# Loading Wk and the first context in three pieces, running the first four K tiles a chunk at a time, and moving Wv ahead of x

## The reference

```
q = LN(x) @ Wq.T + bq;  k = ctx @ Wk.T + bk;  v = ctx @ Wv.T + bv      # 16 heads of 32
x = x + (softmax(q k^T / sqrt(32) + mask) v) @ Wo.T + bo
x = x + self_attention(LN(x))           # q and k RMS-normalised per head
x = x + experts(LN(x))                  # 9 paths, one chosen per token by argmax, then a layer norm
```

## Time and profile before

| | us |
|---|---|
| median of three runs | 752.56 |
| the profiled execution, device time | 751.71 |
| its span, first to last instruction | 749.9 |
| outside the span | 1.81 |
| TensorE busy in the span | 708.2 (94%) |
| VectorE, ScalarE, GpSimd busy | 375.8, 339.7, 197.7 |
| the first matmul starts at | 10.03 |

### The profile page before, as it was taken

How to read it: one execution, slowest core, us unless ns; L and a number is a source line. 1 busy time by engine, 2 the same in 40 slices (tenths; PEclk the granted TensorE clock), 3 DMA queues, 4 the chain that set the end, 5 groups by cost and what they waited for, 6 DMA issues and landing times. The chain is left out here.

```text
span 749.9 us, 20567 instructions
## 1 busy us (share of the span) xinstructions
PE 708.2 (94%) x8150; PEld 550.0 (73%) x8150; DVE 375.8 (50%) x993; ACT 339.7 (45%) x743; POOL 197.7 (26%) x281
## 2 busy tenths in 40 slices
PE   4999999999999999999999999998999989788994
PEld 3777787787788778778778778786787777564662
DVE  5455334424424424425334434576568777581675
ACT  3535534535435434444444443543354544541663
POOL 0001001001001001001000011048776775535755
PEclk9999999999999999999999999999999999989997
DMA  8211110110110110110110211251000005348930
GB/s 332 86 56 58 58 50 9 58 56 0 56 56 0 56 56 0 56 56 0 56 56 5 51 56 38 75 136 10 17 15 28 29 31 199 103 164 303 347 137 31
DMA packets 17557, 55.97 MB, mean 75 GB/s; under 512 B 6098, under 2 KB 6354, under 8 KB 14566
## 3 DMA queue, kind: packets, MB, share of 16 engines
q1 hardware_dynamic: 13926, 40.64, 15.9%
q0 software_dynamic: 3584, 14.69, 5.1%
HBM read 46.93 MB, written 10.49 MB: 77 GB/s over the span
## 5 line engine op out<-in xcount | busy, mean ns | idle before, releaser
L96 PE MATMUL pj<-W_both 128*128 128x512 f32 x544 | 222.1, 408 | 10.1 <-DVE W_both L595 10.0
L98 PE MATMUL pj<-W_both 128*128 128x512 f32 x544 | 213.8, 393 | 0.0
L97 PE MATMUL pj<-W_both 128*128 128x512 f32 x544 | 212.7, 391 | 0.0
L96 PEld LDWEIGHTS pj<-W_both 128*128 128x128 f32 x544 | 102.8, 189 | 43.2 <-issue 23.6
L98 PEld LDWEIGHTS pj<-W_both 128*128 128x128 f32 x544 | 102.6, 189 | 23.0
L236 POOL COPY q_b<-Q_T 128x128 f32 (+1 forms) x32 | 9.3, 290 | 416.3 <-PE tp L359 349.3
L97 PEld LDWEIGHTS pj<-W_both 128*128 128x128 f32 x544 | 103.0, 189 | 19.2
L493 ACT ACTIVATE K<-pj,bk 128x512 f32<-128x512 f32 x64 | 44.1, 689 | 136.4 <-PE pj L98 136.4
L654 DVE CUSTOM_DVE_ANT_0 m_flat<-sc,mask 128x257 f32<-128x257 f32 x64 | 24.7, 424 | 116.5 <-PE tp L359 95.2
L508 ACT ACTIVATE p_flat<-m_flat,nmax 128x257 f32<-128x257 f32 x128 | 63.8, 501 | 25.5 <-DVE nmax L654 25.4
L500 ACT ACTIVATE V<-pj 128x512 f32<-128x512 f32 x64 | 38.2, 596 | 73.3 <-PE pj L98 71.8
(11 more groups left out here) (365 smaller groups left out, 1149.7 us busy)
## 6 DMA issues: line engine op xcount, KB each, us to landing
raw<-ctx_dram SPq DMA_DIRECT2D x15, 1024.0 KB, 4.8
experts<-w_dram SPq DMA_DIRECT2D x6, 768.0 KB, 5.8
raw<-w_dram SPq DMA_DIRECT2D x4, 1024.0 KB, 4.9
x_nat<-x_dram SPq DMA_DIRECT2D x2, 1024.0 KB, 12.1
rows<-z3s SPq DMA_DIRECT2D x8, 256.0 KB, 2.0
rows<-x_nat SPq DMA_DIRECT2D x8, 256.0 KB, 3.1
rows<-xm SPq DMA_DIRECT2D x8, 256.0 KB, 2.2
raw<-wk_dram SPq DMA_DIRECT2D x2, 512.0 KB, 5.7
```

Of the source, the lines that this page charges most:

```text
L96: eng.matmul(out, a_hi, b_hi, start=first, stop=False)
L97: eng.matmul(out, a_lo, b_hi, start=False, stop=False)
L98: return eng.matmul(out, a_hi, b_lo, start=False, stop=last)
```

## The change

The first loads come as a quarter (chunk 0), a quarter (chunk 1) and a half (chunks 2 and 3), each of `Wk` and of context 0 in turn; both splitting engines take the same three pieces. TensorE runs chunk 0 of all four K tiles, then chunk 1 of all four, and then tile by tile chunks 2 and 3. For that the four K tiles have a bank each: `pj[0]`, `pj[1]`, `sc[0]` and `sc[1]`. `Wv` is loaded right after, ahead of `bq`, `bk` and `x`; ScalarE splits it before it empties the first K tile, and VectorE before the layer norm statistics. V tile 0 waits for `Wv` chunk by chunk; V tiles 0 and 1 wait for K tiles 0 and 1 to be emptied, and `tails`, which uses `sc[0]` and `sc[1]` next, for K tiles 2 and 3. Two semaphores get a second use, with their later counts raised to match.

```diff
+        first_k_bank = (pj[0], pj[1], sc[0], sc[1])
-        in_halves = (slice(0, CT // 2), slice(CT // 2, CT))
+        in_parts = (slice(0, 1), slice(1, 2), slice(2, CT))
@@ SyncE
-            for i, half in enumerate((slice(0, CT * D // 2), slice(CT * D // 2, CT * D))):
-                eng.dma_start(raw[:, 1, half], io["wk"][:, half]).then_inc(wk_in[i], 16)
-                eng.dma_start(p_flat[:, half], io["ctx"][0][:, half]).then_inc(ctx_in[0] if i else ctx0_in, 16)
-            eng.dma_start(x_nat[:, 0:4, :], io["x"][:, 0:4, :]).then_inc(x_in[0], 16)
+            for i, cs in enumerate(in_parts):
+                part = slice(cs.start * D, cs.stop * D)
+                eng.dma_start(raw[:, 1, part], io["wk"][:, part]).then_inc(wk_in[i], 16)
+                eng.dma_start(p_flat[:, part], io["ctx"][0][:, part]).then_inc(ctx0_in[i], 16)
+            eng.dma_start(m_flat[:, 0:CT * D], io["wv"]).then_inc(wv_in, 16)
             eng.dma_start(bq[:, :], io["bq"]).then_inc(bias_in, 16)
             eng.dma_start(bk[:, :], io["bk"]).then_inc(bias_in, 16)
-            eng.dma_start(m_flat[:, 0:CT * D], io["wv"]).then_inc(wv_in, 16)
+            eng.dma_start(x_nat[:, 0:4, :], io["x"][:, 0:4, :]).then_inc(x_in[0], 16)
@@ TensorE
+            def first_k(g, c):
+                mm = three(eng, first_k_bank[g][:, :], wk_hi[:, c, g * P:(g + 1) * P], wk_lo[:, c, g * P:(g + 1) * P],
+                           c_hi[0][:, c, :], c_lo[0][:, c, :], c == 0, c == CT - 1)
+                if c == CT - 1:
+                    mm.then_inc(kv_done, 1)
             def v_tile(n, p, t):
-                if isinstance(n, int) and n == 0 and t == 0:
-                    eng.wait_ge(wv_lo_made, CT)
+                start = isinstance(n, int) and n == 0
                 if t < 2:
-                    eng.wait_ge(k_out, 4 * n + 3 + t)
+                    eng.wait_ge(k_out, t + 1 if start else 4 * n + 3 + t)
...
                 for c in range(CT):
+                    if start and t == 0:
+                        eng.wait_ge(wv_lo_made, c + 1)
             def first_pair():
+                for c in range(2):
+                    eng.wait_ge(wk_lo_made, c + 1)
+                    eng.wait_ge(ctx0_lo, c + 1)
+                    for g in range(CT):
+                        first_k(g, c)
+                eng.wait_ge(wk_lo_made, PARTS)
+                eng.wait_ge(ctx_lo, 1)
                 for g in range(CT):
-                    k_tile(0, 0, g)
+                    for c in range(2, CT):
+                        first_k(g, c)
             def tails():
+                    eng.wait_ge(k_out, 3 + i)
@@ ScalarE
-                for i, cs in enumerate(in_halves):
+                for i, cs in enumerate(in_parts):
...
+                eng.wait_ge(wv_in, 16)
+                for c in range(CT):
+                    split_hi(wv_hi[:, c, :].rearrange("p (r g d) -> p r g d", r=4, g=CT), wv_by_tile(c)).then_inc(wv_hi_made, 1)
                 eng.wait_ge(bias_in, 2 * 16)
                 k_evac(0, 0)
                 k_evac(0, 1)
-                eng.wait_ge(wv_in, 16)
-                for c in range(CT):
-                    split_hi(wv_hi[:, c, :].rearrange("p (r g d) -> p r g d", r=4, g=CT), wv_by_tile(c)).then_inc(wv_hi_made, 1)
@@ VectorE
-                layer_norm_stats(0)
-                eng.wait_ge(wv_hi_made, CT)
                 for c in range(CT):
+                    eng.wait_ge(wv_hi_made, c + 1)
                     split_lo(wv_lo[:, c, :].rearrange("p (r g d) -> p r g d", r=4, g=CT), wv_by_tile(c),
                              wv_hi[:, c, :].rearrange("p (r g d) -> p r g d", r=4, g=CT)).then_inc(wv_lo_made, 1)
+                layer_norm_stats(0)
```

More of the change, by code:

```diff
@@ L155, in cross_attention @@
                              "t_lo_made"))
-        ctx0_in, ctx0_hi, ctx0_lo = sem("ctx0_in"), sem("ctx0_hi"), sem("ctx0_lo")
+        first_in, ctx0_hi, ctx0_lo = sem("first_in"), sem("ctx0_hi"), sem("ctx0_lo")
         x_in = [sem(f"x_in{i}") for i in range(2)]
@@ L166, in cross_attention @@
         k_tail, qb_made, wo_in = sem("k_tail"), sem("qb_made"), sem("wo_in")
+        wk_in, ctx0_in = [*wk_in, ctx_in[1]], [first_in, wo_in, ctx_in[0]]
         wk_raw = raw[:, 1, :].rearrange("p (c n) -> p c n", c=CT)
-        in_halves = (slice(0, CT // 2), slice(CT // 2, CT))
+        in_parts = (slice(0, 1), slice(1, 2), slice(2, CT))
+        PARTS = len(in_parts)
         def wv_by_tile(c):
@@ L202, in _ @@
                 eng.dma_start(mask[h * S:(h + 1) * S, :], io["mask"]).then_inc(small_in, 16)
-            eng.wait_ge(wk_lo_made, 2)
+            eng.wait_ge(wk_lo_made, PARTS)
             eng.dma_start(raw[:, 1, :], io["ctx"][1]).then_inc(ctx_in[1], 16)
@@ L308, in tail_transposes @@
                 mm.then_inc(tailT_done, 1)
+            def first_k(g, c):
[3 more added lines that the diff above has]
+                    mm.then_inc(kv_done, 1)
             def k_tile(n, p, g):
-                start = isinstance(n, int) and n == 0
-                if g == 0 and not start:
+                if g == 0:
                     eng.wait_ge(ctx_lo, n + 1)
@@ L320, in k_tile @@
                 for c in range(CT):
[L321 to L326, removed]
                     mm = three(eng, pj[g % 2][:, :], wk_hi[:, c, g * P:(g + 1) * P], wk_lo[:, c, g * P:(g + 1) * P],
@@ L473, in ctx_split @@
             def ctx_split(n, p, i):
-                eng.wait_ge(ctx_in[p], 16 * (i + 1))
+                eng.wait_ge(ctx_in[p], 16 * (i + 1 + p))
                 need(eng, kv_done, 8 * (n - 1))
@@ L482, in weight_split @@
                 if i == 0:
-                    eng.wait_ge(wo_in, 4 * 16)
+                    eng.wait_ge(wo_in, (1 + 4) * 16)
                 else:
@@ L492, in k_evac @@
                     need(eng, s_done, 8 * n)
-                eng.activation(K[:, g, :, 0:SM], pj[g % 2][:, :].rearrange("p (j n) -> p j n", j=2),
+                bank = first_k_bank[g] if isinstance(n, int) and n == 0 else pj[g % 2]
+                eng.activation(K[:, g, :, 0:SM], bank[:, :].rearrange("p (j n) -> p j n", j=2),
                                ACT.Identity, bias=bk[:, g:g + 1]).then_inc(k_out, 1)
@@ L517, in first_pair @@
             def first_pair():
-                for i, cs in enumerate(in_halves):
+                for i, cs in enumerate(in_parts):
                     eng.wait_ge(wk_in[i], 16)
                     split_hi(wk_hi[:, cs, :], wk_raw[:, cs, :]).then_inc(wk_hi_made, 1)
-                    eng.wait_ge(ctx_in[0] if i else ctx0_in, 16)
-                    split_hi(c_hi[0][:, cs, :], ctx0_raw[:, cs, :]).then_inc(ctx_hi if i else ctx0_hi, 1)
+                    eng.wait_ge(ctx0_in[i], 16)
+                    split_hi(c_hi[0][:, cs, :], ctx0_raw[:, cs, :]).then_inc(ctx_hi if i == PARTS - 1 else ctx0_hi, 1)
+                eng.wait_ge(wv_in, 16)
+                for c in range(CT):
+                    split_hi(wv_hi[:, c, :].rearrange("p (r g d) -> p r g d", r=4, g=CT), wv_by_tile(c)).then_inc(wv_hi_made, 1)
                 eng.wait_ge(bias_in, 2 * 16)
@@ L689, in first_pair @@
             def first_pair():
-                for i, cs in enumerate(in_halves):
+                for i, cs in enumerate(in_parts):
+                    last = i == PARTS - 1
                     eng.wait_ge(wk_hi_made, i + 1)
                     split_lo(wk_lo[:, cs, :], wk_raw[:, cs, :], wk_hi[:, cs, :]).then_inc(wk_lo_made, 1)
-                    eng.wait_ge(ctx_hi if i else ctx0_hi, 1)
-                    split_lo(c_lo[0][:, cs, :], ctx0_raw[:, cs, :], c_hi[0][:, cs, :]).then_inc(ctx_lo if i else ctx0_lo, 1)
-                layer_norm_stats(0)
-                eng.wait_ge(wv_hi_made, CT)
+                    eng.wait_ge(ctx_hi if last else ctx0_hi, 1 if last else i + 1)
+                    split_lo(c_lo[0][:, cs, :], ctx0_raw[:, cs, :], c_hi[0][:, cs, :]).then_inc(ctx_lo if last else ctx0_lo, 1)
                 for c in range(CT):
+                    eng.wait_ge(wv_hi_made, c + 1)
                     split_lo(wv_lo[:, c, :].rearrange("p (r g d) -> p r g d", r=4, g=CT), wv_by_tile(c),
                              wv_hi[:, c, :].rearrange("p (r g d) -> p r g d", r=4, g=CT)).then_inc(wv_lo_made, 1)
+                layer_norm_stats(0)
                 z_make(0)
```

## The result

The changed kernel took 745.73 us in the median (745.18 to 747.45, six runs) beside 751.4 us for the kernel before (750.67 to 755.74, six runs): a ratio of 0.9921, 95% interval 0.9898 to 0.9944. That is 5.7 us faster where 3.5 was forecast and under the lowest figure of the range, 747.2. The profiled execution took 745.18 us, with a span of 743.4 against 749.9, 6.5 us less.

A forecast was written before the change was run, and what follows sets the result against it. TensorE's instruction list was taken as the bound, so an earlier start moves everything: 3.34 + 0.18 = 3.52 us gained, giving 748.2 from the profiled execution and 749.0 from the median, middle 748.6; range 747.2 to 749.8.

The forecast's parts named there:

- The first landing, the splits, the first matmul: Kernel start: first quarters usable at 5.21 us, narrower splits save 0.98, first matmul at 6.69, 3.34 us earlier.
- The rise to the full pace: K tiles: TensorE goes from half to full pace 5.26 us after its first matmul, at 11.95.
- the sum: Whole kernel: 3.34 us from the earlier first matmul plus 0.18 before V tile 0, 3.52 us gained.
- Later pieces, `Wv`, z, the extra waits and banks: After the first matmul: all arrive with 2.3 to 4.6 us spare; extra waits and bank changes cost nothing.
- The short wait ahead of V tile 0: Between the last K matmul and V tile 0: the wait for `Wv`'s low part goes, 0.18 us gained.
- whatever starts that list earlier moves all behind it by the same amount: TensorE's whole instruction list: an earlier start carries through to the kernel's end, 3.34 us from the first matmul.
- The lower end: Bottom of the forecast's time range: 747.2 us, with 4.1 + 0.18 us gained from the lower scale.
- small packets: Rival, first loads: each 2 KB packet takes 227 ns, first matmul at 8.3, gain 1.9 us, about 750.2; chance 0.13.
- a late rise: Rival, K tiles: full pace still comes only at 15.29 us, 1.7 plus 0.18 us gained, about 750.2; chance 0.13.
- the best case: First loads: 2 KB packets at 78 ns each, first matmul at 5.9 us, gain 4.1 us.
- The broken start: Rival, K tiles: TensorE stands for each further piece, half pace lasts; 4.0 us later, 756; chance 0.04.

The follow-up runs named there:

- the four repeats: The changed kernel, unedited, run again beside the kernel before: ratios 0.9944, 0.9942, 0.9939 and 0.9924.
- the long hold: The changed kernel with nine GpSimd memsets that TensorE must wait for before its first matmul: 751.56 us beside 752.55 for the kernel before, ratio 0.9989.
- the version with transposes and quarters: The changed kernel plus 24 unused TensorE transposes before the first operands, halves split in quarters, all chunks run across four tiles: 746.26 and 745.69 us.

## Why the prediction was off

- **The first landing, the splits, the first matmul:** right. 5.48 and 6.98 against 5.21 and 6.69; the small pieces cost 0.3 us at the first matmul, not the up to 1.6 of their bound.
- **The rise to the full pace:** that it moves with the first matmul was right; that it took as long in this pair (5.0 us after the first matmul, 5.3 before) was luck. Over all profiles it came 3.5 to 5.3 us after the first matmul in the kernel before and 3.5 to 5.9 in the changed one, which moves V tile 0 by over 1 us (22.45 to 23.69 before, 19.58 to 20.63 after). So the head start of 3.52 us at the 100th matmul, the sum to the digit, was luck too; the mean is 3.2.
- **Later pieces, `Wv`, z, the extra waits and banks:** TensorE waited for none, as forecast, though the second halves, `Wv` and the statistics came 0.7 to 0.9 us later than the sum has them. The short wait ahead of V tile 0 is gone, 0.18 us, too little to be seen in the time.
- **The step that failed** is the first one as the prediction put it: "whatever starts that list earlier moves all behind it by the same amount". It holds to the 6900th matmul (3.6 us). Behind it are stages in which TensorE stands and its clock falls, and what these take varies by up to 5 us between executions of one kernel. The sum took one execution's late stages for fixed, and the range had no term for them: the earlier trace rows stops at 500 us, and I did not price the rest, although the three runs of before lay 4.4 us apart. (The lower end was also 0.2 us too low by its own terms: 751.71 - 4.28 is 747.4.)
- **How much is the change's?** In the profiles the 100th matmul is 3.2 us earlier on average (33.2 of four against 30.1 of five); that is shown, with its mechanism. The medians differed by 3.5 to 6.1 us in five comparisons, and the four repeats average a ratio of 0.9937, 4.7 us, where chance alone was to bring 3.5 (0.995 to 0.996). So about 1 us of the first 5.7 may well be chance of six executions.
- **Is the rest of the excess real?** One by one, the 30 executions of the changed kernel in the repeats took 4.7 us less on average than the 82 of the kernel before on the same chips, with an interval of 0.6 us each way. That is more than the 3.5 forecast and the 3.2 of the start, so chance of the executions doesn't explain it. Part of it is the clock: the mean granted clock of every execution is on record, and within the batches it is higher by 0.0013 (interval 0.0003 to 0.0023) in the changed kernel. Over 750 us that is about 2 us less at half clock, and at the 0.27 us per us found above some 0.5 us. The profiles show the same direction (705.6 us from the 100th matmul to the last in four of the kernel before, 704.2 in five of the changed one), but overlap. About 1 us is left, no more than the uncertainty of a mean head start taken from nine profiles. Why the late stages lose less at half clock is open: they may fall better when they come 3 us sooner, or another part of the change may do it. No run separates these; the long hold, where the gain was gone with the start, fits both, and the version with transposes and quarters, 2 us further ahead, gained only 0.75 us more.
- **The rivals:** small packets came in part, a late rise did not. From 4 to 6 us a 2 KB packet took 0.85 x 16 x 2 us / 132 = 206 ns, near the rival's 227, but by 4.0 us most bytes of the first two pieces were through; the cost was 0.3 us at the first matmul and 0.7 us at the second halves, where it was spare. The 78 ns of the best case was the mean of 887 packets of which 96 carried under 512 B, so a 2 KB packet alone took more. The broken start is real, but needs the tiles in the old order.

## What to carry to other kernels

Cutting the first load into pieces pays only if the tensor engine can do with one piece as much work as the next takes to come: here by opening four accumulators at once; with the old order the same loads made the kernel slightly slower. Look also at the stages in which the tensor engine waits, before calling a shift of the start the whole effect: read the granted clock by windows there, and give the range at least the spread of the runs. One profiled pair is no measure of a change of half a per cent.

## What the hardware showed

The small packets were slower than the large ones in one stretch, and no slower in the next, which holds both sizes. The windows of the changed kernel, against the earlier trace rows; the last column is GB/s:

```profile
2.00:4.00 2.00, 0.00 (x0) 0.00 (x0) 0.78 (x6) 0.07 (x1) 0.00 (x0) 1.00 0.76 215
4.00:6.00 2.00, 0.00 (x0) 0.00 (x0) 0.69 (x1) 1.15 (x2) 0.00 (x0) 1.00 0.85 135
6.00:8.00 2.00, 1.02 (x3) 0.86 (x4) 0.96 (x2) 0.98 (x3) 0.00 (x0) 1.00 1.02 386
```

From 4 to 6 us pieces of 2 KB per partition moved at 135 GB/s, where the pieces of 4 KB of the kernel before moved at 226 in about the same stretch. It was so each time: 109 to 146 GB/s from 4 to 6 us in all thirteen profiles with `Wk` and context 0 in three pieces, 209 to 227 in the five with halves. The second half of context 0 was split at 10.81 instead of 10.12, and at 10.83 to 12.10 in the other twelve. That had slack in the changed kernel, and was the next bound once the half pace was gone. What makes this stretch slow no run shows.
